# A first stage that sums outer products of rows and features, and own buffers in the second output stage

## What is computed

```python
hidden = (x - mean) / sqrt(var + eps)          # per token
k = hidden @ k_w.T + k_b                       # [2048, 512], 16 heads of 32
v = hidden @ v_w.T + v_b
kp = elu(k) + 1.0
kv = einsum('bhsd,bhse->bhde', kp, v)          # per head, over all tokens
ksum = kp.sum(axis=tokens)
```

## Time and profile before

| | us |
|---|---|
| median of three runs | 1527.58 |
| lowest, highest | 1522.91, 1531.15 |
| the profiled execution | 1524.45 |
| its span, first to last instruction | 1522.7 |
| first stage (to PE's first instruction of the next) | 0 to 146.9 |
| second output stage | 1272 to 1328 |

### The profile page before, as it was taken

How to read it: one execution, slowest core, us unless ns; L and a number is a source line. 1 busy time by engine, 2 the same in 40 slices (tenths; PEclk the granted TensorE clock), 3 DMA queues, 4 the chain that set the end, 5 groups by cost and what they waited for, 6 DMA issues and landing times. The chain is left out here.

```text
span 1522.7 us, 23559 instructions
## 1 busy us (share of the span) xinstructions
PE 1459.6 (96%) x6981; PEld 1057.1 (69%) x6981; DVE 1032.7 (68%) x2942; ACT 755.7 (50%) x1283; POOL 464.3 (30%) x697
## 2 busy tenths in 40 slices
PE   6999999999999999999989999999999997998998
PEld 4778788888777888788855555555555555787776
DVE  6453666666658646887867986665668985668592
ACT  5633555655565544433335555555555553234561
POOL 0000577777620112323221222221212214053062
PEclk9999999999999999999979999999999999999999
DMA  5001222222100434376698505315145028743021
GB/s 188 1 1 46 106 92 76 79 110 76 56 28 28 135 108 121 118 202 194 189 238 307 120 6 123 77 53 122 31 97 122 5 81 255 220 168 140 30 82 14
DMA packets 107076, 161.53 MB, mean 106 GB/s; under 512 B 12656, under 2 KB 63744, under 8 KB 100704
## 3 DMA queue, kind: packets, MB, share of 16 engines
q1 hardware_dynamic: 103548, 153.58, 33.5%
q0 software_dynamic: 1024, 2.43, 0.8%
q10 hardware_dynamic: 2404, 4.33, 0.8%
HBM read 117.44 MB, written 42.87 MB: 105 GB/s over the span
## 5 line engine op out<-in xcount | busy, mean ns | idle before, releaser
L2253 ACT ACTIVATE l_pt<-banks 128x1024 f32<-128x1024 f32 (+3 forms) x288 | 218.4, 810 | 140.1 <-PE banks L2124 138.0
L2328 DVE CUSTOM_DVE_ANT_0 stage<-banks,l_edges 128x384 f32<-128x384 f32 (+2 forms) x374 | 197.6, 544 | 79.6 <-issue 78.6
L2164 PE MATMUL banks<-l_pt,l_v 128*64 128x512 f32 (+3 forms) x1152 | 222.0, 507 | 0.4 <-POOL l_pt L2227 0.3
L718 POOL TENSOR_TENSOR ex_hl<-ex_h,ex_hh 128x512 fp32r<-128x512 f32 x128 | 165.3, 1297 | 81.4 <-ACT ex_hh L686 81.3
L2226 POOL TENSOR_TENSOR l_turn<-l_before 128x2 f32<-128x2 f32 x192 | 38.5, 200 | 379.2 <-ACT l_pt L2253 352.5
L751 DVE SCALAR_TENSOR_TENSOR ex_rw<-banks,ex_wb 128x512 f32<-128x512 f32 x128 | 88.3, 691 | 79.0 <-PE banks L75 78.9
L2331 DVE TENSOR_REDUCE l_mx<-banks 128x1 f32<-128x384 f32 (+1 forms) x204 | 111.3, 546 | 33.1 <-PE banks L2102 32.5
L686 ACT ACTIVATE ex_hh<-ex_h 128x512 fp32r<-128x512 f32 x128 | 80.9, 632 | 103.6 <-DVE ex_h L759 102.5
L2164 PEld LDWEIGHTS banks<-l_pt,l_v 128*64 128x64 f32 x1152 | 69.5, 138 | 89.6 <-issue 69.7
L73 PE MATMUL banks<-ex_xlh,ex_wh 128*128 128x512 f32 x256 | 101.6, 397 | 2.0 <-DVE ex_rw L751 2.0
L74 PE MATMUL banks<-ex_xll,ex_wh 128*128 128x512 f32 x256 | 99.8, 390 | 0.0
(11 more groups left out here) (473 smaller groups left out, 3508.2 us busy)
## 6 DMA issues: line engine op xcount, KB each, us to landing
ex_wb<-gates_by_expert SPq DMA_DIRECT2D x16, 1024.0 KB, 4.7
layer_qk<-qkv_yh SPq DMA_DIRECT2D x32, 256.0 KB, 3.2
layer_qk<-qkv_yl SPq DMA_DIRECT2D x32, 256.0 KB, 3.6
layer_v<-qkv_vs SPq DMA_DIRECT2D x15, 512.0 KB, 4.6
l_v<-layer_v SPq DMA_DIRECT2D x7, 1024.0 KB, 17.7
ex_ws<-ew_in SPq DMA_DIRECT2D x16, 384.0 KB, 5.1
l_q<-layer_qk SPq DMA_DIRECT2D x12, 512.0 KB, 7.8
l_k<-layer_qk SPq DMA_DIRECT2D x12, 512.0 KB, 13.8
```

Of the source, the lines that this page charges most:

```text
L718: pool.tensor_tensor(hl[:, k % RING, :], h[:, k % RING, :], raw(hh[:, k % RING, :]), ALU.subtract).then_inc(hl_done, 1)
L2164: last = pe.matmul(bank[h * 2 * HD:(h + 1) * 2 * HD, (qa - b * BT) * P:(qz + 1 - b * BT) * P], v[par][:, kt, h, :], pt[:, step_part(b, j), ...
L2253: act.activation(pt[:, step_part(b, j), :, 0:width], G.banks[:, 2 * slot:2 * slot + 2, 0:width], ACT.Exp, scale=scale).then_inc(p_done, 1)
L2328: dve.tensor_tensor_reduce(cutoff[:, n % 4, 0:width], G.ps[5 + n % MB][:, 0:width], masked, 1.0, NEG, ALU.add, ALU.max, mx[:, h, m, c:c + ...
```

## The change

In the first stage `values`, the value bias addition and `sums_of` go. Each tile's feature matrix `kp` is split (`kh` on ACT, `kl` on DVE), and so are its normalised rows, unturned (`xh`, `xl`, both on GpSimd); ACT now writes the normalised rows over the tokens `X`. `gram(t)` multiplies rows by features in four banks, two tiles behind the keys; keys keep one bank (but for tile 1). GpSimd also sums the features over the tiles (`total`). After the last tile ACT and DVE split the four banks, and `products` multiplies them by the value weights, 48 matmuls of 128 columns, behind four that add the sums times the bias and the ones. The value weights are split at `t = 7` and `9`. The sums' banks are now 6 and 7.

In the second output stage blocks 2 and 3 have inverses of their own (`z2`, `z3`), the stage before puts its output tile `ob` behind its other tiles, SP issues the inverses and outputs of block 2 after two residual tiles, the tables' gathers come after the load of the sums and after the store of the inverses, and DVE takes the reciprocal at `t = 4` instead of 3. `o` and `z` tiles lie in turns in memory, and `ol` of block 3 moves with them.

```diff
@@ -211,26 +211,31 @@
...
+        kh, kl = M.sb("kh", [P, 2, D], F32R), M.sb("kl", [P, 2, D], F32R)
+        xh, xl = M.sb("xh", [P, 2, D], F32R), M.sb("xl", [P, 2, D], F32R)
+        total = M.sb("total", [P, D])
+        gh, gl = (nc.alloc_sbuf_tensor_at("kv_g" + n, [P, NC, D], F32R, offset=G.X_at + at * D * 4)
+                  for n, at in (("h", NT // 2), ("l", NT // 2 + NC)))
         gz, gp = M.sb("gz", [P, NT, EXPERTS]), M.sb("gp", [P, NT, EXPERTS])
@@ -265,11 +273,11 @@
         def _(sp):
...
-            sp.dma_start(vbb[:, :], I["v_b"].partition_broadcast(P)).then_inc(bias_in, 16)
             load_tokens(sp, G, I, 3)
             load_tokens(sp, G, I, 4)
+            sp.dma_start(gb[:, :], I["biases"].partition_broadcast(P)).then_inc(gb_in, 16)
+            sp.dma_start(vbb[:, :, 0:P], I["v_b"].partition_broadcast(P).rearrange("p (g n) -> p g n", g=NC)).then_inc(vb_in, 16)
             weights.load(sp, 4, None)
@@ -283,25 +291,32 @@
...
-                    pe.wait_ge(kx_ready, t - 1)
+                    pe.wait_ge(kx_ready, 1 if t == 2 else t)
                 pe.wait_ge(lo_ready, t + 1)
                 if t == 0:
                     for c in range(NC):
                         pe.wait_ge(weights.w_lo, c // 2 + 1)
-                        last = mm3(pe, pss[K[0]], [(x(0, c), w("k", c))], start=c == 0, stop=c == NC - 1)
+                        last = mm3(pe, key_bank(0), [(x(0, c), w("k", c))], start=c == 0, stop=c == NC - 1)
                     last.then_inc(k_mm, 1)
                 else:
-                    mm3(pe, pss[K[t % 2]], [(x(t, c), w("k", c)) for c in range(NC)]).then_inc(k_mm, 1)
-            def values(t):
-                if t >= 1:
-                    pe.wait_ge(v_ready, t)
-                mm3(pe, pss[V], [(x(t, c), w("v", c)) for c in range(NC)]).then_inc(v_mm, 1)
+                    mm3(pe, key_bank(t), [(x(t, c), w("k", c)) for c in range(NC)]).then_inc(k_mm, 1)
+            def gram(t):
+                if t == 0:
+                    pe.wait_ge(kx_ready, 2)
+                pe.wait_ge(xl_ready, t + 1)
+                pe.wait_ge(kl_ready, t + 1)
+                for c in range(NC):
+                    cols = slice(c * P, (c + 1) * P)
+                    last = mm3(pe, pss[GRAM[c]], [((xh[:, t % 2, cols], xl[:, t % 2, cols]), (kh[:, t % 2, :], kl[:, t % 2, :]))],
+                               start=t == 0, stop=t == NT - 1)
+                last.then_inc(gram_done, 1)
             def logits(b):
@@ -311,35 +326,42 @@
                 mm3(pe, pss[SMALL][0:EXPERTS, :], [(w("g", c), (xTh[:, c, cols], xTl[:, c, cols])) for c in range(NC)]
                     ).then_inc(logit_ready, 1)
-            def sums_of(t):
-                pe.wait_ge(kp_ready, t + 1)
-                pe.wait_ge(v_ready, t + 1)
+            def products():
+                pe.wait_ge(total_ready, NT)
+                pe.wait_ge(vb_in, 16)
+                pe.wait_ge(ones_made, 1)
                 for g in range(NC):
-                    last = pe.matmul(sum_of(g), kp[:, t % 2, g * P:(g + 1) * P], vv[:, t % 2, g, :],
-                                     start=t == 0 and g in (0, NC - 1), stop=t == NT - 1, skip_group_check=True)
+                    pe.matmul(sum_of(g), total[:, g * P:(g + 1) * P], vbb[:, g, :], start=g in (0, NC - 1), stop=False,
+                              skip_group_check=True)
+                weights.ready(pe, 3)
+                for c in range(NC):
+                    pe.wait_ge(gl_ready, c + 1)
+                    wh, wl = w("v", c)
+                    for g in range(NC):
+                        cols = slice(g * P, (g + 1) * P)
+                        last = mm3(pe, sum_of(g)[:, 0:P], [((gh[:, c, cols], gl[:, c, cols]), (wh[:, cols], wl[:, cols]))],
+                                   start=False, stop=c == NC - 1, skip_group_check=True)
                 last.then_inc(kv_done, 1)
             transposes(0)
             keys(0)
             transposes(1)
             keys(1)
-            weights.ready(pe, 1)
             for t in range(NT):
                 if t >= 2:
                     keys(t)
                 if 2 <= t < AHEAD:
                     transposes(2 * t + 2)
                     transposes(2 * t + 3)
-                values(t)
-                if t >= 1:
-                    sums_of(t - 1)
+                if t >= 2:
+                    gram(t - 2)
                 if t < 2:
                     transposes(2 * t + 2)
                     transposes(2 * t + 3)
                 if t % 2 == 1 and t // 2 < NB:
                     if t == 1:
-                        weights.ready(pe, 2)
+                        weights.ready(pe, 1)
                     logits(t // 2)
@@ -356,7 +378,9 @@
                         for k in range(BT):
                             last = pe.transpose(pss[SMALL][0:EXPERTS, k * P:(k + 1) * P], gw[:, b * BT + k, :], G.ident[:, :])
                         last.then_inc(wt_mm, 1)
-            sums_of(NT - 1)
+            gram(NT - 2)
+            gram(NT - 1)
+            products()
@@ -369,9 +393,7 @@
...
-                if t >= RING:
-                    act.wait_ge(xt_ready, t - RING + 1)
-                act.activation(xn[:, t % RING, :], X[:, t, :], ACT.Identity, bias=shift[:, t:t + 1],
+                act.activation(X[:, t, :], X[:, t, :], ACT.Identity, bias=shift[:, t:t + 1],
                                scale=rstd[:, t:t + 1]).then_inc(xn_ready, 1)
@@ -387,6 +409,12 @@
...
+            def feature_high(t):
+                act.wait_ge(kp_ready, t + 1)
+                if t >= 2:
+                    act.wait_ge(gram_done, t - 1)
+                act.activation(kh[:, t % 2, :], kp[:, t % 2, :], ACT.Copy).then_inc(kh_ready, 1)
             root(0)
@@ -406,16 +434,20 @@
                 if t < AHEAD:
                     high(2 * t + 2)
                     high(2 * t + 3)
+                if t >= 1:
+                    feature_high(t - 1)
                 if t + 1 < AHEAD:
                     normal(2 * t + 4)
-                if t in (0, 2):
-                    weights.high(act, 4 + t // 2, 5 + t // 2)
+                if t in (AHEAD, AHEAD + 2):
+                    n = 4 + (t - AHEAD) // 2
+                    weights.high(act, n, n + 1)
                 features(t)
                 if t + 1 < AHEAD:
                     normal(2 * t + 5)
                 if t % 2 == 1 and t // 2 < NB:
                     b = t // 2
                     act.wait_ge(logit_ready, b + 1)
+                    act.wait_ge(xl_ready, b + 1)
                     act.activation(eT(b), pss[SMALL][0:EXPERTS, :], ACT.Exp, scale=-1.0).then_inc(p1, 1)
                 if t == ROOTS:
@@ -425,8 +457,40 @@
...
+                act.activation(gh[:, c, :], pss[GRAM[c]], ACT.Copy).then_inc(gh_ready, 1)
+        @block.gpsimd
+        def _(pool):
+            pool.memset(vbb[:, :, P:W1], 1.0).then_inc(ones_made, 1)
+            def token_split(t):
+                pool.wait_ge(xn_ready, t + 1)
+                if t >= 2:
+                    pool.wait_ge(gram_done, t - 1)
+                pool.tensor_copy(xh[:, t % 2, :], X[:, t, :]).then_inc(xh_ready, 1)
+                pool.wait_ge(xh_ready, t + 1)
+                pool.tensor_tensor(xl[:, t % 2, :], X[:, t, :], raw(xh[:, t % 2, :]), ALU.subtract).then_inc(xl_ready, 1)
+            def feature_total(t):
+                pool.wait_ge(kp_ready, t + 1)
+                if t == 0:
+                    pool.tensor_copy(total[:, :], kp[:, 0, :]).then_inc(total_ready, 1)
+                else:
+                    pool.wait_ge(total_ready, t)
+                    pool.tensor_tensor(total[:, :], total[:, :], kp[:, t % 2, :], ALU.add).then_inc(total_ready, 1)
+            pool.wait_ge(ones_made, 1)
+            token_split(0)
+            token_split(1)
+            for t in range(NT):
+                feature_total(t)
+                if t + 2 < NT:
+                    token_split(t + 2)
         @block.vector
@@ -454,6 +518,12 @@
...
+            def feature_low(t):
+                dve.wait_ge(kh_ready, t + 1)
+                if t >= 2:
+                    dve.wait_ge(gram_done, t - 1)
+                dve.tensor_tensor(kl[:, t % 2, :], kp[:, t % 2, :], raw(kh[:, t % 2, :]), ALU.subtract).then_inc(kl_ready, 1)
@@ -502,25 +571,25 @@
...
-            dve.wait_ge(bias_in, 32)
+            dve.wait_ge(bias_in, 16)
             for t in range(NT):
                 dve.wait_ge(k_mm, t + 1)
                 if t >= 2:
                     dve.wait_ge(r_ready, t - 1)
-                dve.tensor_tensor(kx[:, t % 2, :], pss[K[t % 2]], kbb[:, :], ALU.add).then_inc(kx_ready, 1)
+                dve.tensor_tensor(kx[:, t % 2, :], key_bank(t), kbb[:, :], ALU.add).then_inc(kx_ready, 1)
+                if t >= 1:
+                    feature_low(t - 1)
                 if t < AHEAD:
                     low(2 * t + 2)
                     low(2 * t + 3)
-                dve.wait_ge(v_mm, t + 1)
-                if t >= 2:
```

(47 more changed lines are left out.)

38 lines of the change are left out of this document (20 added, 18 removed).

## The result

| | before | after |
|---|---|---|
| median, us | 1524.99 (20 runs, 1520.57 to 1531.15) | 1531.53 (20 runs, 1528.28 to 1535.25) |
| the profiled execution, us | 1524.45, span 1522.7 | 1533.05, span 1531.3 |
| first stage ends (PE's first instruction of the next), us | 146.87 | 154.14 |
| between the two stages, us | 1125.4 | 1126.8 |
| second output stage (PE's first matmul to the last row addition), us | 54.2 | 54.2 |

The changed kernel is slower: the ratio is 1.0042, 95% interval 1.0035 to 1.005, 6.5 us by the medians. The forecast was 1526.9 and 0.7 us faster than the profiled run of before. The range, 1518 to 1535, holds the time; the chance of "within 0.5%" was the likeliest and holds too, but the direction was wrong.

The account below looks back on a forecast made before the run. TensorE, busy for 96% of the span, was taken as the bound. First stage +4.0 and second output stage -4.7 gave -0.7 us on the profiled 1524.45, 1523.8, forecast as 1526.9 for the timed median; range 1518 to 1535.

Parts of the forecast that it names:

- Opening and tiles 3 to 7: First stage: keys of tile 3 start 1.7 us earlier, then tiles 3 to 7 save 4.7 us in all.
- Gates: First stage, before keys of tile 10: PE stands 4.2 us where it stood 0.8, +3.4 us.
- I take 0.1 us beyond the 1.0: First stage: GpSimd's new work delays DVE by 1.0 us at the opening and only 0.1 us elsewhere.
- The rival on GpSimd: First stage: GpSimd holds up five to six DVE operations at gates, roots and opening, +5 us, 1532; chance 0.12.
- 1.6 us, but the next wait swallows it: First stage, behind the gates' wait: PE's half clock costs 1.6 us, hidden by the next wait, so nothing added.
- roots, turned gates: First stage, tiles 8 to 15: keys 12 wait at the square roots, +1.5 us; turned gates wait 0.6 three times, +1.8.
- End of the stage: First stage's tail: split, 48 small matmuls at 0.12 us and barrier take 7.9 us against 1.8, +6.1.
- Second output stage: Reciprocal wait at block 1 removed, -8.5 us; late residuals and inverses take back 3.8; net -4.7.
- the landing of tile 2: Second output stage: at 292 GB/s residual tile 2 lands at about 1283.7, its add due at 1281; PE waits about 1.8 us.
- the third rival, "the wait moves": Second output stage: block 3's inverses or the residuals take back the whole 6.5 us, 1529.6; chance 0.14.
- a part of the second: Second rival, GpSimd against DVE in the first stage: chain operations held up to 1.3 us each, +5 us, 1532; chance 0.12.
- the output stage still loses more than 5 us to one wait: Second output stage: one of the signs that would prove the prediction wrong; it expected no wait over 3 us at block 1.

Follow-up runs that it names:

- e7: Kernel before with the first stage's change alone, GpSimd also held until DVE's gates are done (waits before tile 8's feature total); 1532.85 us, ratio 1.0055.
- e6: Kernel before with the first stage's change alone, keys of tiles 9 to 15 in three banks and one tile ahead; 1526.6 us, ratio 1.001.
- e14: Kernel before with the output stage's change, first four residual tiles ahead of block 2's inverses, last block's inverses ahead of all gathers, adds in place; 1521.52 us, ratio 0.997.
- e2: Kernel before with the second output stage's part of the change and the moved tile `ob` alone; 1525.69 us, ratio 1.0.
- e4: As e2, but all four first residual tiles issued ahead of block 2's inverses and outputs; 1522.36 us, ratio 0.9984.
- e17: As e14, leaving out half the bytes of residual tiles and stored rows, so half the result isn't computed; 1517.67 us, ratio 0.995.

## Where the prediction failed, and where it held

The direction was wrong: +6.5 us where -0.7 was forecast, with a range wide enough to hold it. Two terms failed. At the gates, TensorE's wait was put at 4.2 us and the half clock behind it at nothing; they were 5.84 and 2.4 us. In the second output stage, residual tile 2 was to land 2 to 3 us late, and DVE stood 9.5 us for it, so the forecast gain of 4.7 was 0.

**Opening and tiles 3 to 7: right.** Keys of tile 8 start at 82.58 in after and at 89.07 in before, 6.5 us earlier; the sum had -1.7 and -4.7. The first low weights took 2.20 us instead of 1.23, held up while GpSimd split token tile 0, as forecast (1.0).

**Gates: place right, size wrong.** This is the term that failed in the first stage. The forecast had PE stand 4.2 us and nothing more; it stood 5.84, and the half clock behind it cost 12 x (0.43 - 0.23) = 2.4 us. Two steps of it were wrong. First, "I take 0.1 us beyond the 1.0": two gate operations were held by GpSimd, 0.95 each, 1.9 us, and e7 got back one of them. The rival on GpSimd named this place, but argued it away from the steady tiles, where DVE has slack; a chain on DVE that PE waits for has none. Second, "1.6 us, but the next wait swallows it": the next wait, at the roots, was forecast at 1.5 and is 0.90, so it swallowed at most the 0.6 and not the 2.4. Together 1.6 + 2.4 of the 3.3 us that the stage missed by; roots, turned gates (0.43 three times, not 0.6) and the end gave back 0.6, 0.5 and 0.4, and 0.8 has no row of its own. e6 shows the place: with other work for PE and the gate operations no longer held, the stage is 5.4 us shorter from there on.

The Trainium skill (SBUF — State Buffer, "SBUF: two separate sides") has a DVE operation with two SBUF inputs and a GpSimd one exclude each other for a whole instruction. By that rule the trace agrees, at 1.37 and 0.42 in one kernel (e7), and here it was worth 1.9 us on PE's path, which the forecast had at 0.1.

**End of the stage: right.** 7.5 us from the last outer product to the next stage against 7.9. The small matmuls follow each other at 0.111 us, by the row of four it was 0.12. By the figure that the Trainium skill gives for 128 columns (TensorE: Matmul & The Clock Gate, "Back-to-back issue gap", 81 ns) they would have taken 3.9 us; they took 5.4.

**Second output stage: the place right, the size wrong.** The forecast let 8.5 us go and took 3.8 back, with residual tile 2 landing 2 to 3 us late. DVE stood 9.5 us for it, and that took the whole gain. The step that failed is the landing of tile 2, worked out as bytes over 292 GB/s. The rate held. The window of after from PE's first matmul of the stage to DVE's addition of tile 2 (last three numbers: clock, DMA share, GB/s), and the queues in it (packets, MB, share of 16 engines; q1 has SP's loads, q0 what GpSimd issues, here mostly gathers, q10 ACT's stores):

```profile
1280.94:1298.14 17.20, 12.56 (x54) 10.03 (x54) 4.48 (x8) 1.90 (x3) 7.51 (x7) 0.97 0.96 284
...
q1 hardware_dynamic: 2157, 3.51, 72.5%
q0 software_dynamic: 320, 0.69, 12.6%
q10 hardware_dynamic: 388, 0.66, 10.7%
```

It took 17.2 us at 284 GB/s, where the forecast had 11.4 (1272.3 to 1283.7). By its own rate that is 3.3 MB; 4.9 MB passed. The sum had too few bytes ahead of the tile: the 2.5 MB named (2.6 in the units here) and the gathers make up the 3.3 alone, and ACT's stores (0.66), tile 2 itself (0.26) and 0.6 MB more on SP's queue are missing. Part of these 0.6 is the last of block 1's inverses, issued by the stage before, for which DVE waits until 1283.02.

The trace shows something else about that queue, which did not decide the landing, since the mean rate was as forecast. Windows of e14 (last three numbers: clock, DMA share, GB/s), first with block 2's inverses at the head of SP's queue, then with outputs and residual tiles there:

```profile
1280.00:1288.00 8.00, 8.00 (x37) 6.57 (x36) 5.70 (x10) 1.90 (x3) 0.79 (x1) 1.00 1.05 260
1288.00:1296.00 8.00, 8.00 (x36) 6.49 (x35) 4.43 (x7) 1.26 (x2) 3.73 (x6) 1.00 1.05 381
```

and of after, with tile 2 in the queue behind the inverses:

```profile
1284.00:1290.00 6.00, 6.00 (x28) 4.97 (x27) 3.79 (x6) 1.65 (x3) 4.78 (x6) 1.00 1.01 239
1292.00:1296.00 4.00, 1.50 (x7) 0.89 (x5) 0.00 (x0) 0.00 (x0) 0.00 (x0) 1.00 1.05 390
```

The engines are full in all four, and move 239 to 260 GB/s while block 2's inverses pass, 381 to 390 behind them. The queues of e14 tell them from the rest, first in 1281 to 1288, then in 1288 to 1295:

```profile
q1 hardware_dynamic: 712, 1.37, 85.6%
q10 hardware_dynamic: 245, 0.47, 18.2%
...
q1 hardware_dynamic: 1359, 2.06, 81.8%
q10 hardware_dynamic: 331, 0.58, 21.6%
```

SP's queue took 4.4 us of all 16 engines per MB in the first and 2.8 in the second, ACT's stores 2.7 and 2.6. Packet by packet in the same trace: of the 2 KB packets of SP's queue, 585 of 798 took over 125 ns between 1278 and 1286 (their median 167), and 23 of 1198 between 1286 and 1295; the others have a median of 84 ns. The 1 MB of inverses makes 512 such packets. Each inverse is read once for many partitions; that this is what makes them slow is not tested, since no run loads them in another way.

So the third rival, "the wait moves" through the residuals (1529.6 for the whole kernel, chance 0.14), had the true course of this stage. It came together with a part of the second, and the forecast priced each alone. The sum, with both terms as measured, is 1525.0 (the median of before over 20 runs, where three had given 1527.6) - 0.7 + 4.7 + 3.3 = 1532.3, against 1531.5.

**The forecast's own test** "the output stage still loses more than 5 us to one wait" decides it: 5.99. It was also a wrong step to take the wait's cost as the gain. Seven kernels removed it; the stage went from 54.2 to 50.7 at best. As the traces read, five transfers and DVE's rhythm of 2.0 us a chunk stand behind each other at nearly the same time, and whichever is put first makes the next one late.

## What to carry to other kernels

Before a wait is taken out, list what else on that queue and on that engine is due within the wait's own length, with its landing time. If several things are, the gain is the distance to the next one, not the wait: here 2.7 to 4.1 us of a forecast 8.5. For a landing, count all that passes until then on all queues, what an earlier stage has left in them too; the mean rate was the safe part of the sum. Where a long chain on one engine holds TensorE, price what other engines will hold in that chain at their full duration, and add the half clock behind the wait in full; what helped was other work for TensorE in free banks (5.4 us in the trace, with both held operations freed by it), far more than one held operation freed (0.95).

## What the runs showed of the chip

- While loads that spread one row over partitions headed SP's queue, the full DMA engines moved 239 to 260 GB/s, against 381 to 390 in the windows behind them; in e14 most 2 KB packets of that queue then took some 167 ns, against 84.
- The Trainium skill (DMA: Bandwidth & Descriptors, "Issuing engines are not separate DMA queues") has transfers of all issuing engines interleave on the same 16 DMA engines. By that rule the traces agree as far as bytes go, but place in one queue still decided which came late: residual tile 2, in kernels with the same transfers, cost DVE 9.1 us behind the inverses and outputs (e2) and nothing ahead of them (e4).
- After a wait of 5.84 us the granted clock was 0.50 until some 5 us after PE had started again; after waits of 2.9 us (e6) and 0.9 us it stayed at 1.00. In e14 two waits of 0.5 and 1.0 us, 2 us apart, were followed by 0.59 and 0.56 in the next two windows of 2 us, but in e17 two waits of 1.0 us, 2 us apart, were not: it stayed at 1.00.
- The length of the unchanged middle of the program varied from 1123.1 to 1127.6 us among profiled runs of kernels that share it, as much as the terms argued over here.
